# Two attention layers with feed-forward parts: two heads packed per block of rows, a new slot order, one Sigmoid pass for the spikes

## The chip, the cores and the metric

The kernel runs on one core of a Trainium2 chip. The metric is the device time of one execution in microseconds (us), a median over several executions. The core has five engines that run their own instruction streams and wait for each other on semaphores: TensorE (PE, whose weight loads are shown apart as PEld), VectorE (DVE), ScalarE (ACT), GpSimd (POOL) and SyncE (SP), which here only issues DMAs.

## What is computed

Two layers on x of 8 batches x 256 rows x 128 columns, each an attention over a context of 256 rows with 16 heads of 8 columns, and then a feed-forward part. Layer 0's feed-forward part is a mixture of eight experts. Layer 1's is a spiking one. Cut to what matters here:

```python
x = x + attention_0(layernorm(x), ctx)          # biases on q, k, v and the output
x = x + experts_0(layernorm(x))                 # one of 8 experts per row
x = x + attention_1(layernorm(x), ctx)          # a bias by position instead
x = x + spikes_1(layernorm(x))

# attention, per batch and head
scores = q @ k.T / sqrt(8)                      # 256 x 256
attn = softmax(scores) @ v                      # 256 x 8
out = concat(attn over heads) @ w_o.T

# spikes_1
y = square(relu(x @ W_fc.T)) @ W_proj.T
for step in range(5):
    reset = (mem > 1); mem = 0.9 * mem + y - reset
    spk[step] = (mem > 1)
result = sum(spk) / 5
```

## The kernel before, in words

One batch is a *block* of two tiles of 128 rows. Each attention layer is a software pipeline of *slots*, s = -3 to 8 (`slots_loop`). In slot b, TensorE multiplies the scores of block b a second time with the row maxima already in the operands (`p2`, written keys by queries into S2), while the maxima of block b+1 are found from a first product (`p1`, queries by keys into S1), block b+2 is projected to q and k, block b+3 is normed, and block b-1 is finished. The names of these cases in the code are `cur`, `nxt`, `new` and `old`.

A slot has eight *pairs* of heads, `pair(0)` to `pair(7)`. In each pair `scores` (L304) issues four `p1` and four `p2` products, each over 32 rows of the array. Head h has the rows 32 (h % 4) and on; the `p2` of a pair belong to the other two row groups. VectorE reduces the `p1` of one head from S1 to its maxima (`reduce`, L656), 128x512 to 128x2; head h uses `S1[h % 2]`, so S1 has one bank per head of a pair. ScalarE takes the exponent of a pair's `p2` in one pass of 128x1024 (L513) into `Pt`. Half way and at the end of the slot the maxima are scaled and split (`shift`, on GpSimd in layer 1), turned by TensorE (`m_turn`), copied by ScalarE (`m_copy`) and written by SP into row 3 of each group of `Qt`.

The value products `pv(b, par, g)` (L338) multiply four heads of group g; each head has a block of 32 rows of the result, of which 9 are used, and so a block of x needs four results of 128x256. They lie in the banks M[0] and M[1], and each is copied to `Osb` by ScalarE (`o_copy`, L500). Then eight transposes (`o_turn`, L367) in two rounds bring them back, VectorE takes the reciprocal of the sums and multiplies (`o_norm`, L672 and L676), two more transposes make `aT`, and the output product L454 is added to X (L763).

Around the pairs the order on TensorE in a steady slot is: pair 0, `pv` of group 3 of block b-1, `m_turn`; pair 1, `o_turn(0)`, turning of the normed x; pair 2, q, `o_turn(1)`; pair 3, k, turning of attn; pair 4, `pv` of group 0 and `m_turn` of the next block; pair 5, v and the output product; pair 6, group 1; pair 7, group 2. ScalarE and VectorE follow the same order, written out by hand.

The feed-forward part of layer 1 (`ffn_on_vector` and its like, from L1352) is a pipeline over blocks of its own. Slot s finds the moments of block s+3 and norms it, multiplies and squares block s+2, projects block s+1, makes the five membrane steps of block s on VectorE (L1369, L1372) and the spikes of block s-1: a Relu pass with bias -1 (L1446), later a Sign pass (L1472), both over 128x1280 on ScalarE; five products with an identity (L1434) add them up. Its first two slots are started inside the last slots of attention (`ffn_start`): the first after pair 4 of slot 7, ahead of `pv` of group 0.

## Time and profile before

| | us |
|---|---|
| median of 3 runs | 438.39 |
| range of the runs | 435.57 to 439.0 |
| profiled execution, own time | 439.88 |
| its span | 438.0 |
| TensorE busy | 344.5 (79%) |
| VectorE busy | 309.1 (71%) |
| ScalarE busy | 268.8 (61%) |
| GpSimd busy | 136.8 (31%) |
| mean granted TensorE clock | 0.878 of 2.4 GHz |

The span is the time from the first to the last instruction of one profiled execution. Busy shares are means over parts with different limits; so the rows further below are cut at the borders of slots (a slot is counted from the start of VectorE's first reduce in it).

### The profile page before, as it was taken

What the parts mean: (1) busy time and instruction counts of PE and PEld (TensorE: products, weight loads), DVE (VectorE), ACT (ScalarE), POOL (GpSimd) and SP (SyncE); (2) the same over time, 40 slices, a digit from 0 to 9 for tenths busy, and PEclk for the clock granted to TensorE, in tenths of its full rate; (3) what the DMA queues carried; (4) which work ended last, traced back from release to release, by engine and by line L of the source; (5) the groups of instructions that cost most, each with busy time, mean ns of one, the idle gap of its engine ahead of it and who ended that gap; (6) DMA issues with size and microseconds to landing.
All of it is one profiled execution on the core that took longest, in us unless ns stands there. A gap on an engine that the chain in (4) does not pass through costs nothing.

```text
span 438.0 us, 9507 instructions
## 1 busy us (share of the span) xinstructions
PE 344.5 (79%) x3230; PEld 205.2 (47%) x3230; DVE 309.1 (71%) x840; ACT 268.8 (61%) x473; POOL 136.8 (31%) x238
## 2 busy tenths in 40 slices
PE   1589999999897625999932679999999888796762
PEld 0233454445343514999920224545444343575751
DVE  5787999998957365466514777999998752268764
ACT  2128988889767201665511148898988785367776
POOL 4423123534002005644037455444642101011000
PEclk9999999999979855899975556999999995889996
DMA  5134342333201402554112122111221000000001
GB/s 150 55 84 127 101 121 67 108 106 88 65 4 53 138 19 43 144 146 100 42 51 67 56 60 59 49 47 49 60 68 56 5 6 1 0 1 13 15 22 48
DMA packets 35920, 27.36 MB, mean 62 GB/s; under 512 B 5936, under 2 KB 31920, under 8 KB 35872
## 3 DMA queue, kind: packets, MB, share of 16 engines
q1 hardware_dynamic: 32896, 23.51, 18.7%
q0 software_dynamic: 1248, 2.56, 2.7%
q10 hardware_dynamic: 1728, 0.66, 0.6%
q8 instruction: 29, 0.48, 0.4%
q14 instruction: 19, 0.16, 0.1%
HBM read 14.19 MB, written 4.13 MB: 42 GB/s over the span
## 4 chain that ended last, share of the span: by engine, by line
PE 55%; DVE 18%; ACT 11%; issue 6%; DMA 5%; POOL 4%; SPq 0%; ACTq 0%; DVEq 0%; POOLq 0%
PE M L338 14%; PE S L287 11%; DVE nm L656 9%; PE S L1234 5%; PE S L1253 4%; ACT Pt L513 3%; PE S L1410 3%; PE M L446 2%; PE M L454 2%; PE M L346 2%; DMA sorted_y<-ysb 2%; PE M L1426 2%; ACT spike L1472 2%; PE M L409 2%; PE S L1434 1%
## 5 line engine op out<-in xcount | busy, mean ns | idle before, releaser
L656 DVE TENSOR_REDUCE nm<-S 128x2 f32<-128x512 f32 x256 | 164.5, 686 | 31.3 <-PE S L287 29.1
L513 ACT ACTIVATE Pt<-S 128x1024 f32<-128x1024 f32 x128 | 130.3, 1019 | 35.8 <-PE S L296 33.7
L287 PE MATMUL S<-Kt,Qt 32*128 32x256 f16 x512 | 86.9, 303 | 18.3 <-DVE nm L656 8.4
L296 PE MATMUL S<-Qt,Kt 32*128 32x256 f16 x512 | 79.1, 290 | 0.0
L338 PE MATMUL M<-Pt,Vt 128*32 128x256 f32 x1024 | 74.5, 412 | 1.5 <-ACT Osb L500 0.9
L287 PEld LDWEIGHTS S<-Kt,Qt 32*128 32x128 f16 x512 | 25.1, 95 | 74.4 <-DVE nm L656 49.1
L338 PEld LDWEIGHTS M<-Pt,Vt 128*32 128x32 f32 x1024 | 28.0, 114 | 29.4 <-issue 6.5
L632 POOL TENSOR_TENSOR rstd<-ve,mhalf 128x2 f32<-128x2 f32 x24 | 17.8, 743 | 63.0 <-DVE ve L610 62.4
L1279 ACT ACTIVATE hf<-S,b1c 128x128 f32<-128x128 f32 x92 | 26.1, 369 | 18.4 <-PE S L1234 18.4
L815 POOL TENSOR_TENSOR q_lo<-qf,q_hi 128x256 f16<-128x256 f32 x15 | 10.1, 671 | 74.5 <-ACT q_hi L546 74.5
L1151 POOL DMA_INDIRECT xt<-normed_x,source x23 | 22.4, 974 | 34.6 <-DVE source L1069 17.0
L1234 PE MATMUL S<-x_t,w_t 128*128 128x128 f32 x184 | 27.7, 298 | 0.0
L296 PEld LDWEIGHTS S<-Qt,Kt 32*128 32x128 f16 x512 | 23.6, 94 | 4.8 <-issue 3.1
L1234 PEld LDWEIGHTS S<-x_t,w_t 128*128 128x128 f32 x184 | 24.8, 209 | 0.4 <-issue 0.2
L1253 PE MATMUL S<-w_ff,hf 128*128 x184 | 24.3, 276 | 0.6 <-DVE ysb L1308 0.6
L535 ACT ACTIVATE xnT<-M 128x256 f32<-128x256 f32 x16 | 6.0, 378 | 29.3 <-PE M L402 26.8
L1253 PEld LDWEIGHTS S<-w_ff,hf 128*128 128x128 f32 x184 | 22.4, 192 | 0.8 <-issue 0.8
L367 PE MATMUL M<-eye,Osb 128*128 128x128 f32 x128 | 20.4, 282 | 2.8 <-DVE attn L676 1.4
L625 POOL TENSOR_SCALAR xn<-X,mv,rstd 128x128 f32<-128x128 f32 x28 | 22.1, 794 | 1.4
L1158 POOL DMA_INDIRECT w_ff<-sorted_y,slot x16 | 15.5, 968 | 21.5 <-DMA sorted_y<-ysb 17.3
L1369 DVE SCALAR_TENSOR_TENSOR tmp<-Pt 128x256 f32<-128x256 f32 x32 | 13.6, 424 | 10.5 <-ACT Pt L1467 9.7
L672 DVE RECIPROCAL rc<-M 128x16 f32<-128x16 f32 x32 | 8.0, 250 | 17.2 <-PE M L367 17.2
(173 smaller groups left out, 574.0 us busy)
## 6 DMA issues: line engine op xcount, KB each, us to landing
w_ff<-in_w SPq DMA_DIRECT2D x8, 512.0 KB, 3.9
ctxT<-in_ctxT SPq DMA_DIRECT2D x16, 128.0 KB, 2.6
Pt<-in_mask SPq DMA_DIRECT2D x8, 256.0 KB, 3.0
Qt<-q_hi SPq DMA_DIRECT2D x28, 64.0 KB, 1.9
Kt<-k_hi SPq DMA_DIRECT2D x28, 64.0 KB, 1.9
sorted_y<-ysb SPq DMA_DIRECT2D x23, 64.0 KB, 2.7
Kt<-k_lo SPq DMA_DIRECT2D x16, 64.0 KB, 1.9
Qt<-q_const SPq DMA_DIRECT2D x16, 64.0 KB, 2.6
```

Of the source, the lines that this page charges most:

```text
L287: mm = pe.matmul(S1[h % 2][:, q, :], Qt[b % NBUF][rows_of(h), h // HG, q * P:(q + 1) * P], Kt[b % NBUF][rows_of(h), h // HG, :], start=Tru ...
L296: mm = pe.matmul(S2[pair % 2][:, hh, k, :], Kt[b % NBUF][rows_of(h), h // HG, k * P:(k + 1) * P], Qt[b % NBUF][rows_of(h), h // HG, :], st ...
L338: mm = pe.matmul(M[O_BANK[g]][32 * i:32 * i + 32, 0:S], Vt[par][:, k, HG * g + i, :], Pt[g][:, i, k * S:(k + 1) * S], start=(k == 0), stop ...
L367: mm = pe.transpose(M[1][:, g * P:(g + 1) * P], Osb[par1][:, g, q * P:(q + 1) * P], eye[:, :])
L513: act.activation(Pt[i // 2][:, 2 * j:2 * j + 2, :].rearrange("p a n -> p (a n)"), S2[i % 2][:, :, :, :].rearrange("p a k n -> p (a k n)"), ...
L625: i = pool.tensor_scalar(xn[par][:, q, :], X[:, b * QT + q, :], mv[:, q, 0:1], rstd[:, q:q + 1], ALU.subtract, ALU.mult)
L632: pool.tensor_tensor(rstd[:, :], ve[:, :], mhalf[:, 0:QT], ALU.pow).then_inc(rst, 1)
L656: v.tensor_reduce(nm[par][:, h // 8, :, h % HG, h // HG % 2], S1[h % 2][:, :, :], AX.X, ALU.max, negate=True)\
L1151: pool.indirect_dma_start(xt[j % XT_BUFS][:, :], None, xn_dram, bass.IndirectOffsetOnAxis(ap=source[:, j:j + 1].bitcast(U32), axis=0)) \
L1234: mm = pe.matmul(S2[j % H_BUFS // 2][:, j % 2, c // 2, (c % 2) * P:(c % 2 + 1) * P], w1_t[j % X_BUFS][:, c, :], x_t[j % X_BUFS][:, :], sta ...
L1253: pe.matmul(o, hf[j % HF_BUFS][:, c * P:(c + 1) * P], second_weights(e, c), start=(c == 0), stop=False)
L1279: i = act.activation(hf[j % HF_BUFS][:, c * P:(c + 1) * P], S2[j % H_BUFS // 2][:, j % 2, c // 2, (c % 2) * P:(c % 2 + 1) * P], ACT.Silu, ...
```

## The change

It has four parts.

- **Packing.** A block of 32 rows of the value product holds two heads: group pairs (0, 1) and (2, 3) are added into the same block of M[1], with V laid out so that the second head's nine columns come 16 further on. The four results are two, side by side in one bank; one copy of 128x512, four transposes in one round, and one reciprocal and multiply over both halves take the place of four copies, eight transposes and two of each.
- **Scores.** In `scores` the wait for the maxima covers both reduces of the pair before, ahead of the first product, and the eight products of a pair are issued in another order: the first key or query half of both heads, then the second.
- **Slot order.** `pv` of group 0 moves behind pair 5 (with `m_turn` of the next block ahead of it), v and the output product move behind pair 4, the addition to X behind reduce 4, the moments behind reduce 5, and the copy of V goes from VectorE to ScalarE, behind pass 4. The keys' copies on ScalarE come ahead of the copy of aT. The first feed-forward slot is started after pair 6.
- **Feed-forward part.** Relu and Sign become one Sigmoid pass with a scale of 1.75 * 2**30; in the last slot it is cut in two. Norming moves from VectorE to GpSimd. The wait for the finished X stands further back on TensorE.

```diff
             def scores(b, i, nxt, cur):
...
-                        if b + 1 > 0 or h >= 2:
-                            pe.wait_ge(ly["max_done"], 16 * (b + 1) + h - 1)
...
-                    for n in range(QT):
...
+                    if b + 1 > 0 or i >= 1:
+                        pe.wait_ge(ly["max_done"], 16 * (b + 1) + 2 * i)
...
+                for n in range(QT):
+                    for hh in range(2):
                         if nxt:
-                            first = p1(b + 1, h, n)
+                            first = p1(b + 1, 2 * i + hh, n)
+                            if n == QT - 1:
+                                first.then_inc(ly["p1_done"], 1)
                         if cur:
                             second = p2(b, i, hh, n)
-                    if nxt:
-                        first.then_inc(ly["p1_done"], 1)
...
+                tile, sub = g // 2, g % 2
                 for k in range(QT):
                     for i in range(HG):
-                        mm = pe.matmul(M[O_BANK[g]][32 * i:32 * i + 32, 0:S], Vt[par][:, k, HG * g + i, :],
-                                       Pt[g][:, i, k * S:(k + 1) * S], start=(k == 0), stop=(k == QT - 1))
+                        at = (k * NPK + tile) * 2 * (HG * KB + KH) + sub * HG * KB + i * KB
+                        mm = pe.matmul(M[1][KB * i:KB * i + KB, tile * S:(tile + 1) * S], Vflat[par][:, at:at + KB],
+                                       Pt[g][:, i, k * S:(k + 1) * S], start=(sub == 0 and k == 0),
+                                       stop=(sub == 1 and k == QT - 1))
...
+                def outputs_turn():
+                    if old:
+                        pe.wait_ge(ly["o_copied"], b)
+                        for n in range(QT * NPK):
+                            q, tile = n // NPK, n % NPK
+                            mm = pe.transpose(M[1][:, n * P:(n + 1) * P], Osb[par1][:, tile, q * P:(q + 1) * P], eye[:, :])
+                        mm.then_inc(ly["ot_done"], 1)
...
                 pair(4)
-                if ffn and s == B - 1:
-                    ffn_start(ffn, -3)
-                if nxt and ly["bias"]:
-                    next_m_turn()
-                if cur:
...
-                    pv(b, par, 0)
-                if nxt and ly["position"]:
-                    next_m_turn()
-                pair(5)
...
                 if old:
...
                     mm.then_inc(ly["op_done"], 1)
...
                     mm.then_inc(ly["v_done"], 1)
+                pair(5)
+                if nxt:
+                    pe.wait_ge(ly["v_copied"], b + 2)
+                    m_turn(b + 1, par1, 0)
                 if cur:
                     if old:
                         pe.wait_ge(ly["x_added"], b)
...
+                    pv(b, par, 0)
+                pair(6)
+                if cur:
+                    pv(b, par, 1)
+                if ffn and s == B - 1:
+                    ffn_start(ffn, -3)
+                pair(7)
+                if cur:
                     pv(b, par, 2)
...
-            def o_copy(b, par, g):
-                act.wait_ge(ly["pv_done"], 4 * b + g + 1)
-                act.activation(Osb[par][:, g, :], M[O_BANK[g]][:, 0:S], ACT.Identity,
+            def o_copy(b, par):
+                act.wait_ge(ly["pv_done"], NG * (b + 1))
+                act.activation(Osb[par][:, :, :].rearrange("p t n -> p (t n)"), M[1][:, :], ACT.Identity,
...
+                exp(4)
+                if nxt:
+                    act.wait_ge(ly["v_done"], b + 2)
...
+                    act.activation(Vheads[1 - par][:, :, :, 0:DH],
+                                   M[0][:, 0:S].rearrange("p (a i d) -> p a i d", i=HG, d=DH), ACT.Copy) \
+                       .then_inc(ly["v_copied"], 1)
                     m_copy(b + 1, 0)
...
                 r(2)
...
-                    o_norm(b - 1, 1)
+                    o_norm(b - 1)
...
-                    v.wait_ge(ly["v_done"], b + 2)
...
-                    v.tensor_copy(Vt[1 - par][:, :, :, 0:DH], M[0][:, 0:S].rearrange("p (k h d) -> p k h d", k=QT, h=H)) \
-                     .then_inc(ly["v_copied"], 1)
...
         def ffn_on_gpsimd(pool):
             for b in range(B):
                 norm_root(pool, b, ff["var"], ff["rstd"])
+                if b >= 2:
+                    pool.wait_ge(ff["xT"], b - 1)
+                norm_apply(pool, b, xn[b % 2], ff["rstd"], ff["xn"])
...
                 if exists(s, -1):
-
-                    act.wait_ge(ff["mem"], 2 * (STEPS - 1) * b)
-                    if not (isinstance(b, int) and b == 1):
-                        act.wait_ge(ff["spike"], b - 1)
-                    act.activation(above[:, :, :], mem[1 - par][:, 0:STEPS, :], ACT.Relu, bias=minus_one[:, :]) \
-                       .then_inc(ff["above"], 1)
+                    if reused(b - 1):
+                        act.wait_ge(ff["count"], b - 2)
+                    cuts = (0, STEPS - 1, STEPS) if s == B else (0, STEPS)
+                    for start, end in zip(cuts, cuts[1:]):
+                        act.wait_ge(ff["mem"], 2 * (STEPS - 1) * (b - 1) + 2 * (end - 1))
+                        act.activation(spike[1 - par][:, start:end, :], mem[1 - par][:, start:end, :], ACT.Sigmoid,
+                                       bias=spike_bias[:, :], scale=SPIKE).then_inc(ff["spike"], 1)
...
-                    act.activation(spike[1 - par][:, :, :], above[:, :, :], ACT.Sign).then_inc(ff["spike"], 1)
```

## Rows read from the trace of the kernel before

**Rows 1.** Busy time per stretch: us, PE, PEld, DVE, ACT, POOL, clock, DMA share, GB/s
```profile
46.47:59.87 13.40, 12.88 (x160) 6.51 (x156) 13.01 (x31) 11.75 (x21) 4.33 (x6) 1.00 0.40 105
287.29:300.78 13.49, 12.86 (x160) 6.53 (x156) 12.76 (x29) 11.97 (x21) 6.99 (x18) 1.00 0.19 55
```
**Rows 2.** Timeline of one pair of heads, slot 3 of layer 0: start, us, instruction
```profile
74.64 0.28 PE L287 MATMUL S<-Kt,Qt 32*128 32x256 f16 x1
74.65 0.28 PE L287 MATMUL S<-Kt,Qt 32*128 32x256 f16 x1
75.06 1.29 DVE L656 TENSOR_REDUCE nm<-S 128x2 f32<-128x512 f32 x2
75.81 0.28 PE L287 MATMUL S<-Kt,Qt 32*128 32x256 f16 x1
76.41 0.28 PE L287 MATMUL S<-Kt,Qt 32*128 32x256 f16 x1 [0.21 <-DVE nm L656]
```
**Rows 3.** Timeline, first pair of slot -1 of layer 0
```profile
17.23 0.61 PE L287 MATMUL S<-Kt,Qt 32*128 32x256 f16 x4 [3.40 <-DMA Qt<-q_lo]
17.86 0.69 DVE L656 TENSOR_REDUCE nm<-S 128x2 f32<-128x512 f32 x1 [2.47 <-PE S L287]
```
**Rows 4.** Busy time per stretch: slots -1, 0 and 6 of both layers
```profile
17.86:32.29 14.43, 11.73 (x48) 4.21 (x48) 12.07 (x26) 2.54 (x6) 4.31 (x6) 1.00 0.23 64
32.29:46.47 14.18, 13.82 (x130) 5.32 (x126) 11.60 (x26) 11.61 (x18) 4.33 (x6) 1.00 0.41 112
240.92:257.37 16.45, 11.49 (x48) 4.20 (x48) 12.56 (x27) 3.64 (x7) 9.37 (x16) 0.50 0.21 63
257.37:273.77 16.40, 14.23 (x130) 5.58 (x126) 11.65 (x24) 11.64 (x18) 7.96 (x19) 0.62 0.19 54
113.44:128.85 15.41, 14.27 (x150) 6.52 (x146) 11.78 (x23) 10.23 (x16) 0.00 (x0) 0.78 0.14 39
341.50:355.60 14.10, 13.02 (x146) 6.06 (x146) 11.51 (x22) 10.07 (x15) 1.70 (x9) 0.88 0.02 6
```
**Rows 5.** Busy time per stretch: slot 7 of layers 0 and 1
```profile
129.00:139.55 10.55, 9.07 (x108) 4.17 (x108) 4.98 (x32) 9.51 (x15) 2.29 (x1) 1.00 0.20 55
355.96:371.27 15.31, 12.68 (x106) 5.45 (x110) 4.49 (x21) 10.26 (x15) 2.25 (x6) 0.70 0.01 3
```
**Rows 6.** Timeline inside slot 7 of layer 1
```profile
362.83 0.69 PE L1418 MATMUL S<-eye,xn 128*128 128x128 f32 x2 [1.61 <-DVE xn L615]
363.45 1.93 PE L338 MATMUL M<-Pt,Vt 128*32 128x256 f32 x16
```
**Rows 7.** Timeline, normalising of the last block of layer 0, both halves
```profile
142.89 0.29 DVE L676 TENSOR_TENSOR attn<-M,rc 128x128 f32<-128x128 f32 x1
144.31 0.29 DVE L676 TENSOR_TENSOR attn<-M,rc 128x128 f32<-128x128 f32 x1
```
**Rows 8.** Busy time per stretch: layer 1 tail, then the feed-forward part
```profile
371.27:381.16 9.89, 7.00 (x48) 4.19 (x40) 1.52 (x6) 3.58 (x7) 0.00 (x0) 0.85 0.00 0
381.16:435.74 54.58, 37.73 (x236) 31.66 (x236) 38.05 (x121) 39.10 (x44) 4.71 (x6) 0.91 0.06 18
```
**Rows 9.** Timeline of ScalarE, one block of the feed-forward part
```profile
404.25 1.27 ACT L1472 ACTIVATE spike<-above 128x1280 f16<-128x1280 f32 x1
405.62 1.36 ACT L1446 ACTIVATE above<-Pt,minus_one 128x1280 f32<-128x1280 f32 x1
410.61 1.27 ACT L1472 ACTIVATE spike<-above 128x1280 f16<-128x1280 f32 x1
```
**Rows 10.** Groups of instructions by line: shapes, count | busy us, mean ns | idle
```profile
L500 ACT ACTIVATE Osb<-M 128x256 f32<-128x256 f32 x32 | 12.2, 381 | 2.9 <-PE M L338 2.9
L625 POOL TENSOR_SCALAR xn<-X,mv,rstd 128x128 f32<-128x128 f32 x28 | 22.1, 794 | 1.4
```
**Rows 11.** Busy time per stretch, for the clock: before a fall, and without one
```profile
116.05:119.47 3.42, 2.65 (x24) 1.11 (x26) 3.35 (x9) 2.07 (x3) 0.00 (x0) 1.00 0.58 163
402.77:406.19 3.42, 1.52 (x15) 1.28 (x14) 2.20 (x10) 3.33 (x5) 0.69 (x1) 1.00 0.13 38
```

More of the change, by code:

```diff
@@ L149, in build @@
         Pt = [sb(f"Pt{i}", [P, HG, QT * S]) for i in range(NG)]
-        Osb = [sb(f"Osb{i}", [P, NG, S]) for i in range(2)]
+        Osb = [sb(f"Osb{i}", [P, NPK, S]) for i in range(2)]
         rc = sb("rc", [P, QT, H])
@@ L551, in slot_fn @@
                 exp(3)
+                if new and not keys_ahead(ly, s):
+                    keys_on_scalar(act, ly, b, nxt)
                 gate = s == B and ly["bias"]
@@ L1352, in ffn_on_vector, with membrane @@
         def ffn_on_vector(v):
[L1353 to L1358 removed]
+            def membrane(b, par):
                 base = 2 * (STEPS - 1) * b
@@ L1362, in membrane @@
                 if reused(b):
-                    v.wait_ge(ff["above"], b - 1)
+                    v.wait_ge(ff["spike"], b - 1)
                 for k in range(1, STEPS):
```

215 lines of the change are left out of this document (86 added, 129 removed).

## The prediction

> **What bounds the kernel now.** I read four views, in this order: busy time per stretch, cut at the slots; the timeline of one slot; the groups by line; and the granted clock. The span is 438.0 us. Most of it is the two layers' attention, in slots of eight pairs of heads. A steady slot takes 13.40 us in layer 0 and 13.49 us in layer 1, five of each kind. In it VectorE is busy 13.01 us (12.76 in layer 1), TensorE 12.88 and ScalarE 11.75 [rows 1]. Two engines are full at once, and they can be so only because the two halves of S1 let them overlap. The timeline shows how. Both heads of a pair start 0.01 us apart (74.64 and 74.65). VectorE starts to reduce them at 75.06. The next pair's first head starts at 75.81, while the second of the two reduces still runs; its second head starts at 76.41, just after they end (75.06 + 1.29 = 76.35) [rows 2].
>
> The feed-forward part is paced otherwise. From one spike pass to the next ScalarE takes 410.61 - 404.25 = 6.36 us [rows 9], while VectorE's work per block is 38.05 / 8 = 4.8 us and ScalarE's 39.10 / 8 = 4.9 us [rows 8]. Each block has a Relu pass of 1.36 us and a Sign pass of 1.27 us over the same data [rows 9].
>
> **The change, part by part.** *The scores' order and wait.* A pair's four score products for the maxima now all wait until both reduces of the pair before are done. So S1 is no longer used in turns: between two pairs' reduces VectorE must wait for a whole round trip. Its parts: from the products' start to the reduce 75.06 - 74.64 = 0.42 us, the two reduces 1.29, from their end to the next products 76.41 - 76.35 = 0.06 [rows 2]. Sum 1.77 us per pair, 14.16 per slot. The other VectorE work lies in gaps of 0.48 us. The sums of x, its moments and the residual addition fit, each about as long as a gap. The joined normalising (its multiply alone was 0.29 us for a half [rows 7]) I bound by 0.3 and 1.1, and take 0.55: 0.07 over the gap. TensorE's work between two pairs is at most 1.6 us, mostly one group of value products, and stays under 1.77, except after pair 4, where the output product waits for ScalarE's copy of aT: 0.05. I get 14.3 us, that is +0.9 in layer 0 and +0.8 in layer 1: 5 x 0.9 + 5 x 0.8 = **+8.5**. That the products stand in two rounds of four gives TensorE nothing: the old order already had both heads side by side when both were free [rows 2], and TensorE is no longer what is waited for.
>
> *What leaves the steady slot.* Three of four copies of O on ScalarE (0.38 us each [rows 10]; the wide one lies between 0.38 and 0.76), four transposes on TensorE, a reciprocal and a multiply, and the V copy, which moves from VectorE to ScalarE and takes 0.4 to 0.6 there. All of it lies beside the round trip: VectorE falls to some 12.2 of 14.3 us, ScalarE to 11.2, TensorE to 12. I cost it at nothing. Without the round trip it would be worth at most 0.8 us a slot on VectorE. Queued behind ScalarE's new wait for the value product are the copy of the maxima and pass 5; their DMA is due at the next slot's pair 0, some 1.4 us later, so nothing is late.
>
> *Slots -1 and 0.* TensorE runs here at half speed though the record gives 1.00 in layer 0: 0.63 us from the products to the reduce [rows 3], so the round trip is 0.63 + 1.29 + 0.06 = 1.98. Eight of them plus 0.4 that the norms after pair 0 take over a gap: 16.2 against 14.43, **+1.8**. In layer 1, where VectorE also adds expert rows: 17.7 against 16.45, **+1.3**. Slot 0: five pairs of 1.98, then value products at half speed behind pairs 5 and 6 (0.43 + 0.4 + 1.9 [rows 6] and 2.1), then 1.8: 16.5 against 14.18, **+2.3**; layer 1, where TensorE waited for x already, **+0.9** [rows 4].
>
> *Slot 6.* Here the clock falls even before: a mean of 0.78 over 15.41 us is 6.8 us at 1.2 GHz [rows 4]. With longer round trips and the V copy's wait in front of the value products, I take 17.0 and 16.1 against 15.41 and 14.10: **+1.6** and **+2.0**.
>
> *Slot 7, no reduces.* In layer 0, 10.55 us [rows 5]; all value products but one now stand behind pair 5, so TensorE has little before them and may drop to 1.2 GHz: 12, **+1.5**. In layer 1 the slot is 15.31 us [rows 5], because the first feed-forward transpose stood in front of the value products, waited 1.61 us for x, and left 1.93 us for each group of sixteen [rows 6]. It now stands behind two groups: also 12, **-3.3**.
>
> *The tails.* One round of turning and normalising goes, 144.31 - 142.89 = 1.42 us [rows 7], with some 0.3 around it: **-1.7** in layer 0. In layer 1 of 9.89 us [rows 8] the copy and the hidden feed-forward product go too: **-2.1**, and the next product no longer waits for the residual: **-0.5**.
>
> *Feed-forward.* One Sigmoid pass (between 1.27 and 1.36 us, the rows of the passes it replaces [rows 9]) takes the place of both, so ScalarE needs some 4.0 us per block. The normalising moves to GpSimd, at 2 x 0.79 = 1.59 us [rows 10], and frees 0.5 on VectorE. Next late is then VectorE with 4.3, and the long way around: moments, root, normalise on GpSimd, transpose, projection, copy, membrane. I estimate it as 3.7 + 0.4 + 1.0 + 0.7 + 1.6 + 0.4 + 1.9 + 0.4 us and eight handovers of 0.06, some 10.6 for two blocks, 5.3 for one. From 6.36 to 5.3 over five blocks is 5.3 us. At the end, after the last membrane step, passes of 1.36 and 1.27 shrink to a short one: 2.5 more. Together **-8.0** (between -5 and -10). The table load lies where ScalarE is idle: 9.89 - 3.58 us of that stretch [rows 8].
>
> By the Trainium skill (SBUF — State Buffer, "Who interferes with whom") GpSimd and a VectorE instruction with two SBUF inputs block each other, which would lengthen GpSimd's part beside the membrane steps. By that rule the saving would be nearer -6; no row here shows this pair of instructions.
>
> The sum: 8.5 + 1.8 + 1.3 + 2.3 + 0.9 + 1.6 + 2.0 + 1.5 - 3.3 - 1.7 - 2.1 - 0.5 - 8.0 = +4.3 us. The profiled execution took 439.88 us, so 444.2 beside it; it was 1.5 above the median of 438.39, from which the sum gives 442.7. I forecast **443**.
>
> **The rivals.** *The clock falls in steady slots too.* Between group 3 and group 0 of the value products there are now four pairs more or less empty. Before, the clock fell at the end of a stretch in which TensorE was busy 2.65 of 3.42 us, with scores and transposes only, and it did not fall with 1.52 us busy of 3.42 with projections and counts [rows 11]. A new steady slot has q and k products in that place, which slot 6 has not; that speaks against. A fall costs at least 15.41 - 13.40 = 2.0 us a slot [rows 1, 4]: in five slots of ten it gives 453, in all ten 463. I give it 0.25. The Trainium skill (TensorE: Matmul & The Clock Gate, "HAM oscillation — how this bites in real kernels") puts the fall down to idle time between bursts of matmuls. By that rule this rival would be nothing, since no such pause arises, and the sum would stand; the trace disagrees with it.
>
> *The slow slots don't lengthen (the other side).* Slots -1, 0, 6 and 7 hold waits already: TensorE is busy 11.5 of 16.45 us and VectorE 12.6 [rows 4]. If these waits, for DMA and GpSimd, absorb the longer round trip, the terms +1.8, +1.3, +2.3, +0.9, +1.6, +2.0 and +1.5 vanish: 442.7 - 11.4 = 431. It decides for faster from some 8.7 us of them on. Against it: in slot -1 of layer 0 VectorE is busy 12.07 of 14.43 us, so only 2.4 us are free. Chance 0.18.
>
> *The round trip is shorter.* If grouping the products took 0.2 us off each (1.57), a steady slot would take 12.6, less than before, and VectorE's own 12.2 would bind next: about -8 instead of +8.5, some 426. It needs under 1.67 to be no loss. The old order measured 0.42 with both heads together [rows 2], and I see nothing to shorten it. Chance 0.10.
>
> **How the numbers follow.** Forecast 0.47 (436 to 449), clock rival 0.25, slow slots 0.18, shorter trip 0.10. The range leaves out the last and the clock rival's upper end, 2 in 10 together: 431 to 458. About 1%, 4.4 us, is what a measurement of this kernel can tell from no change. Faster by more: both rivals on that side, 0.27 of 0.28. Slower by more: the clock rival and 0.25 of the forecast, whose centre lies on that bound: 0.50. Between them 0.23.
>
> **What would show it.** Each pair of reduces in a steady slot starts 1.77 us after the one before; VectorE's idle time in such a slot rises from 13.40 - 13.01 = 0.4 us [rows 1] to some 2. Steady slots take 14.3 us at a clock of 1.00. Slot 7 of layer 1 takes 12 us or less. Spike passes come every 5.3 us. The forecast is wrong if VectorE stays 97% busy in steady slots, if their clock is below 1.00, or if the feed-forward part shrinks by less than 5 or more than 10 us.

## The result and the profile after

The changed kernel takes 452.44 us (median of 4 runs, 451.49 to 455.1), the kernel before 438.69 us beside it (435.57 to 441.89): a ratio of 1.0325, 95% interval 1.0276 to 1.0375. It is slower by 13.75 us where 4.3 were forecast. The profiled execution's span is 450.7 us against 438.0. Ratios leave out the runs that are over 1.5% above the fastest of the same kernel; there are such runs, two of four, in experiments 5 and 6 alone.

From the page of the kernel before, VectorE's score group (line, engine, operation, tiles, count | busy us, mean ns | idle before, releaser) and the chain that ended last by engine:

```profile
L656 DVE TENSOR_REDUCE nm<-S 128x2 f32<-128x512 f32 x256 | 164.5, 686 | 31.3 <-PE S L287 29.1
...
PE 55%; DVE 18%; ACT 11%; issue 6%; DMA 5%; POOL 4%; SPq 0%; ACTq 0%; DVEq 0%; POOLq 0%
```

From the page of the changed kernel, VectorE's and TensorE's score groups and the same chain:

```profile
L648 DVE TENSOR_REDUCE nm<-S 128x2 f32<-128x512 f32 x256 | 165.1, 687 | 60.9 <-PE S L290 59.3
L290 PE MATMUL S<-Kt,Qt 32*128 32x256 f16 x512 | 57.8, 307 | 63.2 <-DVE nm L648 50.2
...
PE 34%; DVE 29%; issue 11%; POOL 9%; ACT 9%; DMA 6%; SPq 1%; POOLq 0%; ACTq 0%; DVEq 0%
```

The two groups wait for each other: VectorE idles 59.3 us ahead of its reduces for TensorE's products (29.1 before), and TensorE 50.2 us ahead of its products for the reduces. That is a round trip, seen from both ends.

Busy time per stretch of the changed kernel (columns as in [rows 1]): a steady slot of layer 0, one of layer 1, the last steady slot of layer 1, slots 7 of both layers, the tail of layer 1, and the feed-forward part.

```profile
51.02:65.56 14.54, 11.08 (x154) 5.38 (x154) 12.38 (x28) 11.41 (x18) 4.33 (x6) 1.00 0.37 105
...
301.99:317.02 15.03, 11.05 (x156) 5.40 (x160) 12.03 (x25) 11.65 (x18) 7.00 (x17) 1.00 0.18 50
347.09:362.97 15.88, 12.52 (x156) 6.26 (x160) 11.34 (x19) 11.41 (x18) 3.38 (x13) 0.89 0.14 38
...
139.71:151.90 12.19, 9.98 (x106) 4.06 (x104) 4.79 (x30) 8.99 (x11) 1.77 (x1) 0.86 0.17 48
378.73:391.02 12.29, 10.31 (x106) 4.17 (x98) 3.05 (x15) 9.48 (x12) 5.00 (x11) 0.86 0.02 5
391.02:397.99 6.97, 5.26 (x39) 3.90 (x40) 1.20 (x4) 4.52 (x7) 0.61 (x1) 1.00 0.00 0
397.99:447.54 49.55, 36.43 (x234) 30.53 (x233) 36.16 (x109) 29.92 (x39) 15.71 (x18) 0.92 0.06 19
```

Set beside [rows 1, 4, 5, 8]: in a steady slot of layer 0 the three busiest engines have less to do than before (TensorE 11.08 us instead of 12.88, VectorE 12.38 instead of 13.01, ScalarE 11.41 instead of 11.75), and the slot is longer, 14.54 us instead of 13.40. None of them is full any more; what takes the time is that they wait for each other. The feed-forward part shrank from 54.58 to 49.55 us, slot 7 of layer 1 from 15.31 to 12.29.

The timeline of two steps of a steady slot of layer 0 (start, us, instruction, idle before):

```profile
61.45 0.28 PE L290 MATMUL S<-Kt,Qt 32*128 32x256 f16 x1
61.87 1.29 DVE L648 TENSOR_REDUCE nm<-S 128x2 f32<-128x512 f32 x2
63.22 0.28 PE L290 MATMUL S<-Kt,Qt 32*128 32x256 f16 x1 [0.38 <-DVE nm L648]
63.65 1.29 DVE L648 TENSOR_REDUCE nm<-S 128x2 f32<-128x512 f32 x2 [0.48 <-PE S L290]
```

Products at 61.45, reduce at 61.87, its end at 63.16, the next products at 63.22, the next reduce at 63.65: 1.77 us a pair. VectorE idles 0.48 us of it with nothing that could start.

By stages, from one execution each (before, after, difference against the prediction's term):

| stage | before | after | difference | forecast |
|---|---|---|---|---|
| start to the first reduce | 17.86 | 18.19 | +0.3 | 0 |
| slots -1, layers 0 and 1 | 14.43, 16.45 | 16.43, 16.96 | +2.0, +0.5 | +1.8, +1.3 |
| slots 0 | 14.18, 16.40 | 16.40, 17.48 | +2.2, +1.1 | +2.3, +0.9 |
| five steady slots, layer 0 | 66.97 | 73.06 | +6.1 | +4.5 |
| five steady slots, layer 1 | 67.73 | 75.60 | +7.9 | +4.0 |
| slots 6 | 15.41, 14.10 | 15.63, 15.65 | +0.2, +1.6 | +1.6, +2.0 |
| slots 7 | 10.67, 15.67 | 12.19, 12.40 | +1.5, -3.3 | +1.5, -3.3 |
| tails | 8.40, 9.89 | 7.80, 6.97 | -0.6, -2.9 | -1.7, -2.1 |
| experts | 93.00 | 93.23 | +0.2 | 0 |
| feed-forward | 54.58 | 49.55 | -5.0 | -8.5 |
| last result to the end of the span | 2.3 | 3.2 | +0.9 | 0 |

The differences add up to the +12.7 us between the two spans. In this table slot 7 starts where the last reduce of slot 6 ends, 0.1 to 0.4 us ahead of the exponential with which the rows of slot 7 begin.

### The profile page after: what moved, and what is told of

Read it like the earlier page. It is cut to its first block, busy times and chain, and to the rows that moved or that the text cites. A ratio compares the mean times of both kernels' runs of the same rounds, so it can differ in the third digit from the quotient of the medians.

```text
span 450.7 us, 9227 instructions
## 1 busy us (share of the span) xinstructions
PE 313.5 (70%) x3166; PEld 187.3 (42%) x3166; DVE 298.4 (66%) x776; ACT 253.8 (56%) x436; POOL 150.7 (33%) x254
## 4 chain that ended last, share of the span: by engine, by line
PE 34%; DVE 29%; issue 11%; POOL 9%; ACT 9%; DMA 6%; SPq 1%; POOLq 0%; ACTq 0%; DVEq 0%
DVE nm L648 17%; PE S L290 8%; PE M L340 6%; PE S L1219 4%; PE S L1238 4%; ACT Pt L505 3%; DVE tmp L1349 2%; PE M L433 2%; DVE Pt L1352 2%; POOL xn L617 2%; DMA sorted_y<-ysb 2%; POOL w_ff L1143 2%; PE M L1405 1%; PE M L349 1%; POOL rstd L624 1%
## 5 line engine op out<-in xcount | busy, mean ns | idle before, releaser
L648 DVE TENSOR_REDUCE nm<-S 128x2 f32<-128x512 f32 x256 | 165.1, 687 | 60.9 <-PE S L290 59.3
L290 PE MATMUL S<-Kt,Qt 32*128 32x256 f16 x512 | 57.8, 307 | 63.2 <-DVE nm L648 50.2
L290 PEld LDWEIGHTS S<-Kt,Qt 32*128 32x128 f16 x512 | 15.7, 96 | 111.9 <-DVE nm L648 82.8
L299 PE MATMUL S<-Qt,Kt 32*128 32x256 f16 x512 | 54.7, 293 | 0.7 <-ACT Pt L505 0.7
L1219 PE MATMUL S<-x_t,w_t 128*128 128x128 f32 x184 | 26.7, 291 | 0.0
L1219 PEld LDWEIGHTS S<-x_t,w_t 128*128 128x128 f32 x184 | 23.8, 202 | 0.5 <-issue 0.2
L513 ACT ACTIVATE mT<-M 64x256 f16<-64x256 f16 x32 | 11.9, 373 | 10.7 <-PE M L349 10.3
L1293 DVE COPY ysb<-S 128x128 f32<-128x128 f32 x23 | 6.6, 289 | 16.5 <-PE S L1239 9.2
L299 PEld LDWEIGHTS S<-Qt,Kt 32*128 32x128 f16 x512 | 15.1, 94 | 5.7 <-issue 3.4
```

Source lines behind the costliest of these rows:

```text
L290: mm = pe.matmul(S1[h % 2][:, q, :], Qt[b % NBUF][rows_of(h), h // HG, q * P:(q + 1) * P], Kt[b % NBUF][rows_of(h), h // HG, :], start=Tru ...
L299: mm = pe.matmul(S2[pair % 2][:, hh, k, :], Kt[b % NBUF][rows_of(h), h // HG, k * P:(k + 1) * P], Qt[b % NBUF][rows_of(h), h // HG, :], st ...
L648: v.tensor_reduce(nm[par][:, h // 8, :, h % HG, h // HG % 2], S1[h % 2][:, :, :], AX.X, ALU.max, negate=True)\
L1219: mm = pe.matmul(S2[j % H_BUFS // 2][:, j % 2, c // 2, (c % 2) * P:(c % 2 + 1) * P], w1_t[j % X_BUFS][:, c, :], x_t[j % X_BUFS][:, :], sta ...
```

## The experiments

Twelve kernels ran, in three groups of four; each group had its own runs of the kernel before (medians 437.04, 439.3 and 439.86 us). Unless said otherwise, slot lengths are from the profiled executions.

**1. The new scores function alone, in the kernel before.** It brings the joint wait and the two rounds of four together; all else is before.

```diff
-                        if b + 1 > 0 or h >= 2:
-                            pe.wait_ge(ly["max_done"], 16 * (b + 1) + h - 1)
...
+                    if b + 1 > 0 or i >= 1:
+                        pe.wait_ge(ly["max_done"], 16 * (b + 1) + 2 * i)
...
+                for n in range(QT):
+                    for hh in range(2):
```

> The kernel before with the new score function alone (joint wait for both reduces, two rounds of four). Theory 1: steady slots go from 13.40 us to 14.3 to 15.0, the whole from 438.7 to 452 to 460 us, more than the whole change costs, since the savings elsewhere are missing. Theory 2: 437 to 442 us.

Measured: 454.19 us, ratio 1.0381 (1.0321 to 1.0442). A steady slot, and the feed-forward part:

```profile
65.51:79.84 14.33, 11.52 (x160) 5.91 (x164) 13.02 (x31) 11.73 (x20) 4.33 (x6) 1.00 0.33 96
...
396.19:450.81 54.62, 37.73 (x236) 31.68 (x236) 38.09 (x121) 39.11 (x44) 4.72 (x6) 0.91 0.06 18
```

VectorE has the same 13.0 us of work as in [rows 1] and needs 14.33 us for it instead of 13.40; all five steady slots of layer 0 are like that, at a clock of 1.00. So this function alone costs as much as the whole change: 3.8% against 3.3%, with intervals that overlap. The other parts of the change together give little back: the profiled spans are 453.1 us here and 450.7 in the changed kernel, of which the feed-forward part alone is 54.62 and 49.55.

**2. The changed kernel without the joint wait.** The function scores is the old one.

> The changed kernel with the score function of the kernel before: each head's products wait for the reduce of its own bank only, and a head's two halves follow each other. Theory 1 (the joint wait, a round trip of 1.77 us per pair, makes attention slower): steady slots of layer 0 fall from 14.54 us to 12.8 to 13.4, the whole to 432 to 439 us. Theory 2 (the joint wait is harmless; the packed results, the V copy on ScalarE or the new slot order stretch the slots): steady slots stay at 14.2 to 14.6, the whole at 448 to 453.

Measured: 443.19 us, ratio 1.0144 (1.0085 to 1.0204), between the two theories. That is 1.8% below the changed kernel, so the old function takes back more than half of the cost, yet still slower than before although the feed-forward saves its 5 us here too (49.06 us). Three of the five steady slots of layer 0 take 13.72 and 13.97 us, against 13.40; one of the others holds a fall of the clock (15.35), and the last (14.85) is explained with experiment 8. The timeline around the output product, TensorE and ScalarE:

```profile
82.77 0.47 ACT L477 ACTIVATE kf<-M,qkbs 128x256 f32<-128x256 f32 x1
83.27 0.42 ACT L482 ACTIVATE k_hi<-kf 128x256 f16<-128x256 f32 x1
83.59 0.36 ACT L556 ACTIVATE aT<-M 128x256 f32<-128x256 f32 x1
84.01 0.71 PE L434 MATMUL M<-wo,aT 128*128 128x128 f32 x4 [0.72 <-ACT aT L556]
```

TensorE stands 0.72 us in front of the output product, because the copy of aT waits behind the two copies of the keys (0.47 and 0.42 us) on ScalarE. Pair 5's products stand behind it in TensorE's queue. This place in the new slot order thus has a cost of its own; experiments 8 and 9 show how much of it the joint wait hides.

**3. The changed kernel with the old order of the products.** The joint wait stays.

```diff
-                        if b + 1 > 0 or h >= 2:
-                            pe.wait_ge(ly["max_done"], 16 * (b + 1) + h - 1)
+                        if hh == 0 and (b + 1 > 0 or i >= 1):
+                            pe.wait_ge(ly["max_done"], 16 * (b + 1) + 2 * i)
```

> The changed kernel with its joint wait, but the products in the old order, four rounds of two (both halves of a head, then the other head). If the order is worth nothing and the wait is the whole cost: as the changed kernel, 451 to 454 us, pairs 1.77 us apart. If two rounds of four shorten the products: pairs some 0.1 to 0.2 us further apart and 6 to 15 us slower than the changed kernel.

Measured: 454.01 us, ratio 1.0394 (1.0329 to 1.046); four of the five steady slots of layer 0 are 14.55 to 14.57 us, the changed kernel's 14.54 and 14.55.

So under the joint wait the two rounds of four are worth nothing, and the cost of experiment 1 is the wait's. The rounds without that wait were not tried.

**4. The moments of the next norm earlier.** They stand behind reduce 4, ahead of the addition onto X.

```diff
                 r(4)
+                if ahead and cur:
+                    norm_moments(v, b + 3, ly["norm_own"], ly["xvar"], applied(b + 3))
...
                 r(5)
-                if ahead and cur:
-                    norm_moments(v, b + 3, ly["norm_own"], ly["xvar"], applied(b + 3))
```

> The changed kernel with the moments back behind reduce 4 on VectorE (ahead of the addition to X) instead of behind reduce 5. Theory 3 (in layer 1 GpSimd's chain root, norm, expert mix starts after the moments and makes the split maxima of the next slot late, so that TensorE waits ahead of pair 1): steady slots of layer 1 fall from 15.03 to 14.6 us, layer 0 stays at 14.54 or gets 0.3 longer; whole 449 to 452. Rival (the distance from pair 0 to pair 1 there is the round trip with the sums of x in it): layer 1 stays at 15.0 or above, whole 452 to 455.

Measured: 454.65 us, ratio 1.0417 (1.0343 to 1.0492), no gain. Slots of layer 1 stay at 15.03 to 15.04 us, and those of layer 0 become 14.66. In layer 1 the theory was right about the wait, and the time went elsewhere: the step from pair 0 to pair 1 fell from 2.18 to 1.77 us, and the one behind reduce 4, where the moments and the addition onto X now share a gap, rose from 1.77 to 2.19 (in layer 0 from 1.84 to 1.97). Two pieces of work in one gap of the round trip overflow it.

**5. The feed-forward's start behind pair 6, alone, in the kernel before** (TensorE's part of the edit; ScalarE's follows it).

```diff
                 pair(4)
-                if ffn and s == B - 1:
-                    ffn_start(ffn, -3)
...
                     pv(b, par, 1)
+                if ffn and s == B - 1:
+                    ffn_start(ffn, -3)
                 pair(7)
```

> The kernel before with one edit: the start of the feed-forward in slot 7 of layer 1 (the transposes of its first norm) stands behind pair 6 and value product 1 on TensorE and behind exponential 6 on ScalarE, as in the changed kernel, instead of behind pair 4. Theory (the stall of 3.3 us in that slot delays exponentials and nothing else uses it): slot 7 of layer 1 becomes 12.4 us from 15.7, and the time falls by 3 us, a ratio of 0.993. Rival (the stall only moves: the feed-forward needs its norm at the same moment, so its first membrane step starts later by what the slot saves): slot 7 is shorter, the stretch from the last add onto X to the end is longer by as much, ratio 1.000.

Measured: 437.04 us, ratio 0.9879 (0.9778 to 0.998). The medians, 437.04 and 439.3 us, are 0.5% apart, so the times alone leave open how large the gain is, and barely show it. The stage does show it: from the first reduce of slot 6 of layer 1 to the last addition onto X it takes 36.57 us, against 39.66 before, and 35.43 to 35.68 in experiments 6, 7 and 12, which have the same edit. Slot 7 by itself went from 15.31 [rows 5] to 13.79 us here and to 11.06 in experiment 7; much of that difference is where the clock fell, in slot 7 here and in slot 6 there:

```profile
358.05:371.84 13.79, 12.52 (x111) 5.41 (x112) 4.49 (x21) 10.27 (x15) 2.24 (x6) 0.75 0.01 4
```

The feed-forward part behind it stayed at 53.98 us (54.58 before), so the stall did not merely move.

**6. and 7. The feed-forward part alone, with the norms on GpSimd or on VectorE.** Both are the kernel before with the late start, the changed kernel's Sigmoid pass and its later wait for the finished X; experiment 7 has the norms back on VectorE:

```diff
-                norm_apply(pool, b, xn[b % 2], ff["rstd"], ff["xn"])
...
+                    if k == 2 and new:
+                        apply(b + 3, 1 - par)
```

> The kernel before, with the late start of the feed-forward and the changed kernel's whole feed-forward (one Sigmoid pass, norm on GpSimd); attention is untouched. Theory (the parts of the change add up): 3 us from the start and 5 us from the feed-forward, so about 429 us, a ratio of 0.982; the stretch from the last add onto X to the last result is about 49.5 us as in the changed kernel. Rival (the 5 us come from an attention tail that ended otherwise, not from the Sigmoid pass): at most 2 us beyond the late start, ratio 0.99.

> The kernel before, with the late start and the Sigmoid pass, but the feed-forward's norms stay on VectorE (pairs of 0.34 us) instead of going to GpSimd (pairs of 0.93 us each beside the membrane steps). Theory (the detour over GpSimd delays the first blocks and stretches both engines): 1 to 2 us faster than the same kernel with the norms on GpSimd, the first membrane about 6.5 us behind the last add onto X instead of 7.3. Rival (VectorE sets the pace between membranes, so each norm on it costs its 0.7 us): 2 to 4 us slower than with the norms on GpSimd.

Measured: 430.55 us, 0.9736 (0.9635 to 0.9837; the medians alone give 0.980), and 427.69 us, 0.9738 (0.967 to 0.9805). The two times can't be told apart by their ratios; the stretch from the last addition onto X to the last result can, 50.04 us on GpSimd and 46.70 on VectorE (1 to 2 us less were expected):

```profile
377.20:427.24 50.04, 36.40 (x234) 30.71 (x233) 36.09 (x109) 29.95 (x39) 15.60 (x18) 0.91 0.06 19
```

```profile
358.59:369.65 11.06, 9.55 (x111) 4.51 (x112) 4.40 (x21) 9.92 (x16) 2.26 (x6) 1.00 0.02 4
378.59:425.29 46.70, 35.86 (x235) 29.62 (x234) 37.86 (x120) 29.59 (x37) 5.00 (x6) 0.94 0.07 21
```

VectorE's extra work, 37.86 - 36.09 = 1.8 us in all, costs less than the detour: it is the rival's price that did not come. Where the detour bites is the beginning. The changed kernel, from the first norm of the part to the first membrane step:

```profile
399.92 1.57 POOL L607 TENSOR_SCALAR xn<-X,mv,rstd 128x128 f32<-128x128 f32 x2 [0.18 <-POOL rstd L624]
401.54 0.44 PE L1395 MATMUL S<-eye,xn 128*128 128x128 f32 x2 [2.28 <-POOL xn L607]
401.82 2.99 PE L1405 MATMUL M<-wpr,Pt 128*128 128x128 f32 x16
405.25 0.43 DVE L1349 SCALAR_TENSOR_TENSOR tmp<-Pt 128x256 f32<-128x256 f32 x1 [3.28 <-ACT Pt L1449]
```

and the same steps in experiment 7:

```profile
380.41 0.60 DVE L615 TENSOR_SCALAR xn<-X,mv,rstd 128x128 f32<-128x128 f32 x2 [0.88 <-POOL rstd L632]
381.07 0.44 PE L1416 MATMUL S<-eye,xn 128*128 128x128 f32 x2 [0.38 <-DVE xn L615]
381.34 1.95 PE L1426 MATMUL M<-wpr,Pt 128*128 128x128 f32 x16
383.75 0.43 DVE L1369 SCALAR_TENSOR_TENSOR tmp<-Pt 128x256 f32<-128x256 f32 x1 [1.78 <-ACT Pt L1470]
```

GpSimd needs 1.57 us for what VectorE does in 0.60, and TensorE waits 2.28 us for it. Behind this pause the clock fell (granted 0.50 from 402.5 to 405.9), so that the projection took 2.99 us instead of 1.95. The first membrane step comes 7.26 us behind the last addition onto X (397.99 to 405.25) against 5.16 (378.59 to 383.75). From there to the last result both need nearly the same, 42.3 and 41.5 us; before it was 47.8.

How much of the detour is the clock's can be read from the other kernels with the norms on GpSimd. In six of the eight profiles the clock fell right behind this pause, and the way to the first membrane step took 7.0 to 7.9 us. In the other two (experiments 3 and 10) it had fallen earlier and was back at 1.00 for the projection: there the way took 6.24 us, and the whole part 48.4. So the norm's way itself costs some 1.1 us at the start and 1.7 in all (48.4 - 46.70), and the fall behind the pause up to 1.6 more. That the pause brings on the fall is not shown; it followed it in all six.

**8. aT ahead of the keys on ScalarE, without the joint wait.** The kernel of experiment 2 with this edit:

```diff
                 exp(3)
+                if new and old:
+                    act.wait_ge(ly["aT_done"], b)
+                    if older:
+                        act.wait_ge(ly["op_done"], b - 1)
+                    act.activation(aT[:, :], M[1][:, 0:S], ACT.Copy).then_inc(ly["aT_copied"], 1)
                 if new and not keys_ahead(ly, s):
                     keys_on_scalar(act, ly, b, nxt)
...
-                if old:
+                if old and not new:
                     act.wait_ge(ly["aT_done"], b)
```

> The changed kernel with the old scores function (the kernel of the first experiment, ratio 1.014) and one more edit: ScalarE copies aT ahead of the keys' copies. Theory (the new slot order costs because TensorE waits at the output product for that copy, 0.7 us a slot): steady slots of layer 0 without a clock fall go from 13.97 to about 13.4 us, and the ratio to about 1.004. Rival (the wait moves on to the values' product, which needs the keys' copies, or the spacing of the products between pairs is what costs): slots stay at 13.9 to 14.0, ratio 1.012 to 1.016.

Measured: 434.81 us, ratio 0.9886 (0.9799 to 0.9972), where experiment 2 had 1.0144; forecast was 1.004.

```profile
73.81:87.08 13.27, 12.40 (x152) 5.80 (x152) 12.44 (x27) 11.24 (x18) 4.63 (x7) 1.00 0.33 91
```

```profile
79.90 0.38 ACT L551 ACTIVATE aT<-M 128x256 f32<-128x256 f32 x1
80.16 0.48 ACT L477 ACTIVATE kf<-M,qkbs 128x256 f32<-128x256 f32 x1
80.38 0.71 PE L434 MATMUL M<-wo,aT 128*128 128x128 f32 x4
```

The output product starts right behind the copy, and three of the five steady slots of layer 0 are 13.26 to 13.28 us, the shortest of that layer but for experiment 11's like ones. One place in a queue was worth 0.7 us a slot. The rest of the gain over experiment 2 is in part two falls of the clock fewer (one instead of three).

Another steady slot of layer 0 takes 14.10 us at a clock of 1.00. The step from its pair 0 to its pair 1 is 2.40 us instead of 1.60, because the turn of the maxima waits for VectorE's small scaling of them, which took 1.06 us instead of 0.18. It ran beside a memset that GpSimd does once, in this slot, for the experts. The changed kernel has the same pair in the same slot, where the step is 2.12 instead of 1.77 us:

```profile
94.01 0.95 POOL L1069 MEMSET b2rows<- 128x1024 f16 x1
94.06 0.93 DVE L656 TENSOR_SCALAR mparts<-nm 128x16 f16<-128x16 f32 x1
```

In the kernel before, the memset starts 1.4 us ahead of the scaling, which takes 0.18 us. The slots of 14.2 us in layer 1 of experiment 8 have GpSimd's late maxima parts instead, as in experiment 10 (a step of 2.65 us where the last slot has 1.74).

**9. The same edit in the changed kernel,** with its joint wait.

> The changed kernel with one edit: ScalarE copies aT ahead of the keys' copies, the edit that took 0.7 us from a steady slot of the kernel with the old scores function. Theory (in the changed kernel the round trip between TensorE and VectorE, 1.77 us a pair, sets the pace, and TensorE's order between the pairs has slack below it): steady slots of layer 0 stay at 14.5 us and the ratio at 1.03. Rival (the two costs add): slots of 13.9 us and a ratio of 1.01.

Measured: 450.7 us, ratio 1.0227 (1.0154 to 1.0301). Steady slots of layer 0 take 14.48 us (14.54 without the edit), those of layer 1 15.03 as before. Of the 0.7 us only 0.06 are left: the round trip covers the rest. The ratio is lower than the changed kernel's by more than these slots explain; in this profile the clock did not fall in a steady slot, and the intervals of 1.0227 and 1.0325 overlap.

**10. GpSimd mixes the experts' sums earlier, in the changed kernel.** In layer 1 the changed kernel's step from pair 0 to pair 1 takes 2.18 us (reduces at 317.02 and 319.20) where the others take 1.77:

```profile
316.27 0.72 POOL L1318 TENSOR_TENSOR X<-X,w_ff 128x256 f32<-128x256 f32 x1
...
318.21 0.22 POOL L778 TENSOR_TENSOR mparts<-mr,mparts 128x16 f16<-128x16 f32 x1
318.58 0.27 PE L349 MATMUL M<-eye,mparts 128*64 128x128 f16 x2 [0.56 <-POOL mparts L778]
```

```diff
+                if ly["position"] and 0 <= s < B - MIX:
+                    mix_on_gpsimd(pool, b + MIX)
                 if 0 <= s <= B - 4:
                     norm_root(pool, b + 3, ly["xvar"], ly["xrstd"])
...
-                if ly["position"] and 0 <= s < B - MIX:
-                    mix_on_gpsimd(pool, b + MIX)
```

> The changed kernel with one edit: in slots 0 to 3 of layer 1 GpSimd mixes the experts' sums (0.61 and 0.72 us) ahead of the next norm's root, where it idles 2.0 us, instead of at the end of its slot ahead of the maxima parts. Theory (the 2.18 us step from pair 0 to pair 1 in layer 1, against 1.77 in layer 0, comes from GpSimd's parts being late for TensorE's maxima turn, since the mix stands ahead of them): the step goes to 1.8 us, slots 2 to 4 of layer 1 from 15.03 to 14.6 us, the time falls by 1.3 us. Rival (that step is late for the query tile's DMA or the norm's sums): slots stay at 15.0 us.

Measured: 453.43 us, ratio 1.0307 (1.022 to 1.0395), no gain in the time, where 1.3 us were expected. The slots say why; three in a row of layer 1, and the fourth is like the second (14.61 us):

```profile
289.02:304.88 15.86, 12.49 (x156) 6.35 (x160) 12.13 (x25) 11.42 (x18) 7.01 (x18) 0.89 0.17 47
304.88:319.50 14.62, 11.14 (x156) 5.41 (x160) 12.04 (x25) 11.41 (x18) 7.01 (x18) 1.00 0.18 51
319.50:335.38 15.88, 12.52 (x156) 6.24 (x160) 12.13 (x26) 11.42 (x18) 7.01 (x18) 0.89 0.16 46
```

Where the clock held, a slot takes 14.62 us instead of 15.03, as GpSimd's parts were in time (reduces at 317.43, 319.50, 321.27: that step is 1.77). In two of the four the clock fell, and each of these took 1.25 us longer. So the late parts are the cause of the longer step; what their repair gives in time isn't shown.

**11. All three repairs of the changed kernel:** old scores function, aT first, norms on VectorE.

> The changed kernel with three edits: the old scores function, aT copied ahead of the keys, and the feed-forward's norms back on VectorE. Theory (the costs are separate places and add): 3 us below the kernel with the first two edits (ratio 0.989), so 0.981, and the stretch from the last add onto X to the last result goes from 49.1 to about 46.5 us. Rival (the norms' gain is lost in the attention slots of layer 1): ratio 0.987 to 0.99.

Measured: 430.2 us, ratio 0.9761 (0.9671 to 0.985). The feed-forward part is 46.69 us (46.70 in experiment 7), where experiment 8 had 49.07. That is 2.4 of the 5.9 us between the two spans; 2.1 more lie between the last reduce of layer 0 and the first of layer 1, which the edit does not touch.

**12. The end over two banks.** The kernel of experiment 7, with the spikes of block 6 counted into S1[0], where VectorE's result of that block reads them:

```diff
-                    if not (isinstance(b, int) and b == 1):
+                    if s == B:
+                        pe.wait_ge(ff["out"], b - 2)
+                    elif s != B - 1 and not (isinstance(b, int) and b == 1):
                         pe.wait_ge(ff["out"], b - 1)
...
-                        mm = pe.matmul(S1[1][:, 0, :], eye16[:, :], spike[1 - par][:, k, :], start=(k == 0),
+                        mm = pe.matmul(S1[0 if s == B - 1 else 1][:, 0, :], eye16[:, :], spike[1 - par][:, k, :], start=(k == 0),
```

> The kernel before with the late start, the Sigmoid pass and the norms on VectorE (ratio 0.974), and one more edit: the spikes of block 6 are counted into the bank S1[0], so that this product waits for no result, and the count of block 7 waits for the result of block 5 only. Theory (the end is serial over one bank: fin 5, count 6, fin 6, count 7, fin 7): the stretch from the last membrane step to the last result falls from 4.0 us to about 2.5, the time by 1.5 to 1.8 us, a ratio of 0.970. Rival (the last Sigmoid passes end as late as the counts do): less than 0.4 us.

Measured: 427.91 us, ratio 0.9687 (0.9612 to 0.9762). The end of the changed kernel, where every count waits for a result and every result for a count, each count at half clock (1.23 us against 0.71 for the block before):

```profile
444.02 1.23 PE L1413 MATMUL S<-spike,eye 128*128 128x256 f16 x5 [3.18 <-DVE fin L1360]
445.29 0.42 DVE L1360 SCALAR_TENSOR_TENSOR fin<-S,X 128x256 f32<-128x256 f32 x1 [1.41 <-PE S L1413]
445.86 1.22 PE L1413 MATMUL S<-spike,eye 128*128 128x256 f16 x5 [0.61 <-DVE fin L1360]
447.12 0.42 DVE L1360 SCALAR_TENSOR_TENSOR fin<-S,X 128x256 f32<-128x256 f32 x1 [1.41 <-PE S L1413]
```

and of this experiment:

```profile
422.87 0.75 DVE L1382 SCALAR_TENSOR_TENSOR fin<-S,X 128x256 f32<-128x256 f32 x2
423.73 1.25 PE L1436 MATMUL S<-spike,eye 128*128 128x256 f16 x5 [2.15 <-ACT spike L1451]
425.26 0.42 DVE L1382 SCALAR_TENSOR_TENSOR fin<-S,X 128x256 f32<-128x256 f32 x1 [1.64 <-DMA out<-fin]
```

Two results now follow the last membrane step directly, and from its end to the last result it takes 2.7 us instead of 4.0. The next in line shows at once: the last result waits for the DMA that empties its buffer. The gain of 1.3 us is shown in the trace alone. The ratios of experiments 7 and 12 overlap, and the whole part takes 46.15 us against 46.70, since in this profile the way to the first membrane step took 5.87 us at a mean granted clock of 0.68, instead of 5.16 at 0.89.

## Why the forecast was right in kind and short in size

**The round trip: right.** The step of 1.77 us per pair was put together from three rows of [rows 2], and it is what the profile after shows, to 0.01 us. VectorE's idle time in a steady slot rose from 0.4 to 14.54 - 12.38 = 2.2 us (forecast: some 2). The steady slot of 14.3 us is what the new scores function alone gives (14.33, experiment 1), and without it the slots fall to 13.3 once aT is copied first (experiment 8). That the two rounds of four give nothing under the joint wait is experiment 3.

**Where the number fell short.** The change of 13.75 us is three times the sum of 4.3. The measured 452.44 us lies above the 436 to 449 of the forecast itself, and inside the stated range only through the room left for a clock that falls in five slots or more. It fell in one, for 1.3 us. That the range held is in part luck: other terms filled that room.

**Steady slots of layer 0: +6.1 instead of +4.5.** A slot of 14.54 us has five steps of 1.77 and three longer ones: 1.93 us at the joined normalising, 1.85 where the output product stands, and 1.91 at the slot's end. Together they are 0.38 us over, where I had 0.12. Two terms fell short. The normalising takes 0.35 + 0.43 = 0.78 us where I took 0.55, inside the bounds I gave (0.3 to 1.1). The slot's end, 0.14 over, I had put at nothing; it is 1.91 in experiment 1 too, so it comes with the joint wait and not with the new order.

```profile
55.77 0.35 DVE L664 RECIPROCAL rc<-M 128x32 f32<-128x32 f32 x1
56.15 0.43 DVE L668 TENSOR_TENSOR attn<-M,rc 128x256 f32<-128x256 f32 x1
```

One of the five slots had 0.35 us more, for the scaling beside GpSimd's memset (experiment 8).

**Steady slots of layer 1: +7.9 instead of +4.0.** The step that failed is the one that took layer 1 to be like layer 0. GpSimd's parts are late in layer 1, where it also mixes the experts' sums. Now that the next products wait for both reduces and for this turn one behind the other, the lateness is on the path: 0.41 us in each of three slots, shown by experiments 4 and 10. Why it cost next to nothing before (probably the slack of the two halves of S1) was not tried. Another 1.3 us is a fall of the clock in the last steady slot, and the rest, 0.3 us a slot, is again the normalising (1.93) and the slot's end (2.07).

**The clock rival: it happened, but rarely.** The prediction gave it 0.25 and placed it in five slots or all ten; it came in one of ten. Its price was too high as well: 1.25 us a fall (experiment 10) instead of 2.0, which had been read from slot 6 against a steady slot, two slots with different work. In the ten steady slots of a profiled execution the clock fell in no slot of the six kernels with the old attention order (before, experiments 1, 5, 6, 7 and 12). With the changed one it fell in 1 (after), 3, 1, 2, 1, 0, 3 and 0 slots (experiments 2, 3, 4, 8, 9, 10 and 11), with the joint wait and without it: 11 of 80 slots against 0 of 60. So something in the changed attention makes it possible, and the scores function alone does not (experiment 1). Which part of it does, the order of the slot, as the rival said, or the packing, was not tried apart. Nine of the eleven falls begin 7.3 to 8.6 us into the slot, about where the output product stands, the other two at 4.4 and 4.5. In the 3 us ahead of a fall no pause of TensorE is longer than 0.8 us in nine of them (0.67 in the changed kernel), and up to 1.2 in the other two. The Trainium skill (TensorE: Matmul & The Clock Gate, "HAM oscillation — how this bites in real kernels") puts falls down to idle time between bursts of matmuls, by which none would come here; the trace disagrees.

**The feed-forward: -5.0 instead of -8.5.** The mechanism was right, the sizes of three terms were not. (a) I had the first block gain 0.5 us; it lost 0.5 (7.26 us against 6.78 from the last addition onto X to the first membrane step), for the norm's way over GpSimd and the fall of the clock behind it (experiments 6 and 7). (b) The pace between membranes was taken as 5.3 us and is 5.47 over four blocks, so the stretch of membranes shrank by 4.75 us instead of 5.3. The prediction had set beside its sum the rule of the Trainium skill (SBUF — State Buffer, "Who interferes with whom") that GpSimd and a VectorE instruction with two SBUF inputs block each other. The trace agrees with it: a pair of norm instructions on GpSimd takes 1.57 us alone and 1.88 beside the membrane steps, and a membrane step 0.56 instead of 0.42:

```profile
411.05 1.88 POOL L607 TENSOR_SCALAR xn<-X,mv,rstd 128x128 f32<-128x128 f32 x2 [0.18 <-POOL rstd L624]
412.30 0.56 DVE L1352 SCALAR_TENSOR_TENSOR Pt<-Pt,tmp 128x256 f32<-128x256 f32 x1
```

(c) The end was taken as 2.5 us shorter and is 0.8 shorter: I counted the shorter passes on ScalarE and overlooked that two counts and two results pass through one bank one after the other; experiment 12 gets 1.3 us of it. The terms as written add up to 8.3 us, the sum had 8.5. With the norms left on VectorE the part shrinks by 54.58 - 46.70 = 7.9 us, nearly what I had forecast for it with them on GpSimd; the agreement of that number is chance.

**Slots -1, 0, 6 and 7, and the tails.** Slots -1 and 0 were +5.8 against +6.3, with steps of 1.99 us where 1.98 was forecast. Slots 7 came as forecast, though layer 1's took 12.3 us where "12 or less" was the sign, and experiments 5 to 7 show the late start as a gain by itself. Slots 6 were +1.8 against +3.6. In layer 0 it was +0.2: that slot had steps of 3.34 and 2.55 us before and has two of 2.55 now, with the clock down for 6.8 us both times. In layer 1 it was +1.6, and there the clock was down for 6.8 us instead of 3.4. Tails -3.5 against -3.8. The start, the experts and the end after the last result, which had no term, were +1.4. The rival that said the slow slots would not lengthen is dead (+9.1 for its seven terms); so is the one with a shorter round trip.

**What the parts are worth.** By spans of the profiled executions: the changed kernel 450.7; without the joint wait 440.8; with aT ahead of the keys 433.4; with the norms on VectorE 427.5, and the kernel before with only the new feed-forward part and its late start, norms on VectorE, 427.6. So packing two heads and the new slot order bring nothing that can be measured over the old attention, once the joint wait and the late copy of aT are mended, and the gain comes from the Sigmoid pass and the late start. The best versions are those of experiments 7, 11 and 12, 2.4 to 3.1% below the kernel before; their intervals overlap, so they can't be ranked.

## What to carry to other kernels

Where two engines work at each other's heels over two halves of a buffer, joining the waits of both halves turns an overlap into a round trip. Add up the round trip from the timeline before touching anything: the step came out to 0.01 us here, while the slot of eight steps was missed by 0.24, through the work that no longer fits between them. A round trip then hides other mistakes (a copy behind the wrong ones in a queue was worth 0.06 us under it and 0.7 without), so that the parts of a change must be tried both with and without each other. A part moved to an engine with time to spare still lengthens the chain it is in: look at where the chain starts and ends, where nothing overlaps it.

## What the hardware showed

- Equal work does not get an equal clock. In experiment 10 two slots of layer 1 have the same instructions at the same distances, to 0.03 us; these are the same 3.4 us of each:

```profile
293.10:296.50 3.40, 1.72 (x22) 0.82 (x21) 2.88 (x7) 3.34 (x8) 1.15 (x4) 1.00 0.14 42
308.98:312.38 3.40, 1.72 (x22) 0.85 (x21) 2.88 (x7) 3.34 (x8) 1.17 (x4) 1.00 0.17 49
```

  Behind the first the granted clock fell from 2.4 to 1.2 GHz (0.50, from 296.5 to 299.9), behind the second it stayed. So whether it falls is not settled by what TensorE did in that stretch alone, and a profile of one execution shows only one draw: such slots are better counted over several kernels.
- A fall of 3.4 us inside a slot that is bound by the round trip costs 1.25 us (14.62 to 15.88), although TensorE has 3.5 us to spare in it.
- The granted clock of the record can't be taken as the speed at the start of this kernel. In slot -1 of layer 0 the record gives 1.00, yet a score product lasts 0.40 us (median), as in slot -1 of layer 1 at 0.50, and 0.27 in the steady slots.
- A small VectorE instruction that ran beside a GpSimd memset of 0.95 us took 0.93 to 1.37 us instead of 0.18 (the changed kernel, experiments 2, 3, 8, 9 and 11), and both ended within 0.04 us of each other.
- One Sigmoid pass over 128x1280 takes 1.36 us, as one of the two passes it replaces; its table load of 1.28 us stood in a gap of ScalarE.
